# Issuing half of the output stores from ScalarE, half from SyncE, in a vision tower kernel on one core

## What is computed

```python
tokens = layernorm(patches, ln1_g, ln1_b) @ W1 + b1
tokens = layernorm(tokens, ln2_g, ln2_b)
tokens = jnp.concatenate([tokens, tokens, tokens], axis=1)      # (4, 3 * 784, 64)
h = silu(layernorm(tokens @ Wp1 + bp1, lnp_g, lnp_b)) @ Wp2 + bp2
h = h + gated_layer(layernorm(h))
h = h + experts_4(layernorm(h))
# attention, 8 heads of rank 32
scores = einsum('bhtr,bhur->bhtu', q, k) / sqrt(64)
h = h + einsum('bhtd,hde->bte', softmax(scores) @ x, VO)
# experts 1 to 8, the best two weighted
for e in range(8):
    y = gelu(tokens @ w1[e] + b1[e], approximate=False) @ w2[e] + b2[e]
    out = out + combine[:, e:e + 1] * y
return h + out                                                   # (4, 2352, 64)
```

## Time and profile before

| | before |
|---|---|
| median of 3 runs | 721.47 us (716.13 to 722.4) |
| the profiled execution, device time | 709.28 us |
| its span, first to last instruction | 707.5 us |
| outside of the span | 1.8 us |
| TensorE busy | 639.1 us, 90% of the span |
| VectorE, ScalarE, GpSimd busy | 425.3, 353.6, 66.7 us |
| mean granted TensorE clock | 0.972 of full speed |

### The profile page before, as it was taken

How to read it: one execution, slowest core, us unless ns; L and a number is a source line. 1 busy time by engine, 2 the same in 40 slices (tenths; PEclk the granted TensorE clock), 3 DMA queues, 4 the chain that set the end, 5 groups by cost and what they waited for, 6 DMA issues and landing times.

```text
span 707.5 us, 10081 instructions
## 1 busy us (share of the span) xinstructions
PE 639.1 (90%) x3032; PEld 334.3 (47%) x3032; DVE 425.3 (60%) x1028; ACT 353.6 (50%) x538; POOL 66.7 (9%) x76
## 2 busy tenths in 40 slices
PE   0795888997969999999999999999999999978993
PEld 0552444544435555545555555555555554446431
DVE  3845456125857676676677676677676775187451
ACT  0547885648524445445445445455445455568211
POOL 0000000001990010010010010010110100100000
PEclk9998899999979999999999999999999999999997
DMA  7400000001521232231221322322322310000024
GB/s 154 189 0 1 0 0 1 0 1 46 137 63 50 63 75 65 68 84 50 73 77 50 79 71 50 84 65 50 87 62 56 93 50 2 1 1 0 1 51 85
DMA packets 22112, 37.83 MB, mean 53 GB/s; under 512 B 5624, under 2 KB 15288, under 8 KB 21832
## 3 DMA queue, kind: packets, MB, share of 16 engines
q1 hardware_dynamic: 21944, 37.32, 20.8%
q10 hardware_dynamic: 144, 0.20, 0.2%
HBM read 6.27 MB, written 2.61 MB: 13 GB/s over the span
## 4 chain that ended last, share of the span: by engine, by line
PE 86%; DVE 5%; ACT 3%; DMA 3%; SPq 1%; issue 1%; DVEq 0%; ACTq 0%
PE P L662 83%; DMA X<-x 2%; PE P L678 1%; ACT L472 1%; DVE xs L1218 1%; ACT rs L472 0%; PE P L908 0%; PE P L1020 0%; SPq L351 0%; PE P L782 0%; DVE xhat L1158 0%; DVE mx L1328 0%; DVE gate_s L1206 0%; SPq L355 0%; SPq L356 0%
## 5 line engine op out<-in xcount | busy, mean ns | idle before, releaser
L572 ACT ACTIVATE PT<-P 112x784 f32<-112x784 f32 x224 | 184.4, 823 | 215.6 <-PE P L662 215.5
L1328 DVE TENSOR_REDUCE mx<-P 112x1 f32<-112x392 f32 x448 | 243.1, 563 | 80.6 <-PE P L662 80.5
L662 PE MATMUL P<-PT,XVs 112*64 112x392 f32 x896 | 197.4, 519 | 0.2
L662 PE MATMUL P<-Ks,Qs 96*112 96x392 f32 x448 | 171.4, 387 | 1.8 <-DMA Ks<-QKH 1.1
L662 PEld LDWEIGHTS P<-Ks,Qs 96*112 96x112 f32 x448 | 77.4, 175 | 118.3 <-DVE mx L1328 111.6
L662 PE MATMUL P<-Qs,Ks 98*112 98x392 f32 x448 | 118.6, 346 | 6.8 <-DMA Qs<-row_store 6.8
L662 PEld LDWEIGHTS P<-Qs,Ks 98*112 98x112 f32 x448 | 78.4, 178 | 15.3 <-issue 13.1
L662 PEld LDWEIGHTS P<-PT,XVs 112*64 112x64 f32 x896 | 44.4, 135 | 61.7 <-issue 60.9
L662 PEld LDWEIGHTS P<-VBs,CT 128*98 128x98 f32 x320 | 34.8, 165 | 20.2 <-issue 19.0
L1355 DVE RECIPROCAL zi<-P 98x1 f32<-98x1 f32 x32 | 5.4, 168 | 63.5 <-PE P L662 63.5
L662 PE MATMUL P<-VBs,CT 128*98 128x130 f32 (+1 forms) x320 | 39.2, 269 | 0.6 <-ACT CT L579 0.6
(11 more groups left out here) (178 smaller groups left out, 599.9 us busy)
## 6 DMA issues: line engine op xcount, KB each, us to landing
Qs<-QKH SPq DMA_DIRECT2D x64, 98.0 KB, 2.1
Ks<-QKH SPq DMA_DIRECT2D x64, 98.0 KB, 2.2
XVs<-XV SPq DMA_DIRECT2D x32, 196.0 KB, 2.5
Qs<-QKL SPq DMA_DIRECT2D x32, 98.0 KB, 2.1
Ks<-QKL SPq DMA_DIRECT2D x32, 98.0 KB, 2.1
X<-x SPq DMA_DIRECT2D x4, 588.0 KB
out<-OT SPq DMA_DIRECT2D x24, 98.0 KB
wa<-table_a SPq DMA_DIRECT2D x1, 2207.5 KB, 8.2
```

The costliest lines, as they stand in the source:

```text
L572: nc.scalar.activation(PT[:, p, :].rearrange("p (c n) -> p c n", c=2), P[0:T, 2 + 2 * p:4 + 2 * p, 0:HALF], ACT.Exp, scale=float(D) ** -0. ...
L662: return nc.tensor.matmul(dst, lhsT, rhs, start=start, stop=stop, **more)
L1328: nc.vector.tensor_reduce(mx[:, s % 2, c, t:t + 1], bank(c if n is None else n)[0:T, :], AX.X, ALU.max)\
```

## The change

The view of the output is made once, ahead of the engines' blocks, under the name `out_rows`. SyncE keeps the three stores of `j = 0` of each image. The three stores of `j = 1` go to ScalarE's code, right behind the image's two copies, with a wait for ScalarE's own last copy ahead of them. There are 24 stores as before, of the same sizes and to the same places. SyncE still waits for all of them at the end.

```diff
+        out_rows = out.rearrange("b (k i h j cd) d -> b i k h j (cd d)", k=REP, i=NP, h=2, j=OJ)
+
         @block.sync
...
-            rows = out.rearrange("b (k i h j cd) d -> b i k h j (cd d)", k=REP, i=NP, h=2, j=OJ)
             for b in range(B):
                 sync.wait_ge(hid_done, HID["out", b, 1] + 1)
-                for j in range(OJ):
-                    for k in range(REP):
-                        sync.dma_start(rows[b, :, k, :, j, :], OT[j * NP:(j + 1) * NP, b, :, :]).then_inc(stored[b], 16)
+                for k in range(REP):
+                    sync.dma_start(out_rows[b, :, k, :, 0, :], OT[0:NP, b, :, :]).then_inc(stored[b], 16)
...
             for b in range(B):
                 for part in range(2):
                     rows_out_of(b, part)
+                scalar.wait_ge(hid_done, HID["out", b, 1] + 1)
+                for k in range(REP):
+                    scalar.dma_start(out_rows[b, :, k, :, 1, :], OT[NP:2 * NP, b, :, :]).then_inc(stored[b], 16)
```

## The result

| | before | after |
|---|---|---|
| median of 22 runs | 721.67 us (704.48 to 729.11) | 718.84 us (712.57 to 723.57) |
| ratio of medians | | 0.9961 |
| profiled execution | 709.28 us | 718.65 us |
| its span | 707.5 us | 716.8 us |
| mean granted TensorE clock in it | 0.972 | 0.951 |

The comparison of the two kernels gives the ratio 1.0153 (95% interval 1.0102 to 1.0204), so 1.5% slower, while the medians of the same runs say 0.4% faster; it counts only runs within 1.5% of the fastest of their kernel, and these are 2 of the 22 runs of before (704.48 and 709.73 us) against 21 of 22 after.

A forecast was written before the change was run, and what follows sets the result against it. TensorE, busy 639.1 of 707.5 us, bounds the kernel; only the tail can change. Image 3's stores from 698.58, packets 1.6 us later, then 0.9 us: span 704.2, gain 3.3; 721.47 - 3.3 = 718.2 us, range 712.5 to 723.5.

The forecast's parts named there:

- Where the time can change: End of the program: only the 9.4 us behind ScalarE's last copy, 1.3% of the span, can answer to the change.
- the tail: End of the program: from the end of image 2's second copy to the span's end, 12.5 us before the change.
- Images 0 and 1: ScalarE's stores after these images: 2.6 us of issues fit in 7.37 us of idleness, so no gain or loss.
- The delay of image 3's copies: ScalarE after image 2: three issues end at 697.57 us, copies start 0.43 us late, rows ready 0.45 us later.
- The DMA engines decide: Last stores: at a DMA share of 0.9, packets and not issues set the end, 704.2 us, a gain of 3.3.
- Rival A: Last stores: SyncE's and ScalarE's issues exclude each other, image 3's copies wait; span 708.5 us, 1.0 us slower; chance 0.10.
- Rival B: Last stores: packets slow down when two queues feed them, share stays 0.56; span 0.3 us slower, no change; chance 0.10.
- Rival C: Last stores: cheap ScalarE issues, packets overlap fully, issues alone set the end at 702.9 us, gain 4.6 us; chance 0.10.
- The step that failed: From profile to median: the same 3.3 us gain applied 12.2 us higher; scatter alone could pass 1%, slower given 0.03.

## Why the prediction was right and wrong

- **Where the time can change.** Right: the tail only. The changed kernel's profile differs elsewhere, but by the clock, which the kernel before shows alike.
- **Images 0 and 1.** Right: ScalarE's next copy of image 1 still follows 7.37 us of idleness.
- **The delay of image 3's copies.** Forecast 0.43 us, measured 0.56: an interval of 0.89 us on ScalarE, not 0.86. I called it the cost; the kernels that avoid it with stores of this form have longer tails (10.1, 10.4 and 10.2 us).
- **The DMA engines decide.** Right, but the share was 0.79, not the 0.9 taken, so the last packets took 3.4 us and not 3.2. With the later copies this makes the tail 9.6 us where 9.2 was forecast (704.2 less 694.97), a gain of 2.9 us where 3.3 was. By its own terms (698.58 + 1.6 + 3.2 + 0.9) the sum gives 704.3 and not 704.2 us, which changes nothing.
- **Rival A**, the queues exclude each other, is refuted: 0.820 us on SyncE with ScalarE issuing beside it and without, and 0.852 us on ScalarE, with SyncE issuing beside it and, in the kernel with all stores on ScalarE, without. The lock wait that the Trainium skill describes ("Perfetto Trace Analysis", section "DMA Instruction — HWDGE (DVE, Sync)") does not show in these lengths. Rival A's other half, copies queued behind issues, is real, as all stores on ScalarE show.
- **Rival B** is refuted: the DMA share rose from 0.56 to 0.79. The Trainium skill ("DMA: Bandwidth & Descriptors", section "Issuing engines are not separate DMA queues") says that several issuing engines save only issuing time, usually little. The trace agrees that it is issuing time that is saved, but here that is not little: issuing was 0.82 us for a store whose packets need about 0.5 us of the DMA engines, and where issuing was made cheap on one queue, the second queue gained nothing (8.6 against 9.0 us).
- **Rival C**, no bound by the DMA engines, did not come.
- **The time.** 718.2 us was forecast, the median is 718.84 us. Both medians, of the 3 runs known then and of the 22 after, are of the common group of runs, and that they are is luck: the sum did not know of the groups.
- **The step that failed.** The comparison came out at 1.0153, beyond 1% on the slower side, to which I gave 0.03. The step is the last sentence of the sum, "Against the median of the runs, 12.2 us higher, the same gain", with the statement under chances that "no mechanism gives 7.2". I took the 12.2 us between the profiled execution and the median as an offset and the runs as scatter around one value. They are two groups some 12 us apart, set by 10 or 37.5 us of the lower clock near 195 us, and the profiled execution was of the rare one. Each splits by another 5 to 6 us, as 716.13 us among the three runs could have told. The mechanism outside the change that moves a run by 1.7% was in the profile's distance to its own runs, and I did not ask what it was. A comparison that takes the rare group for one kernel and the common one for the other shows that group's distance, less the gain. Why the clock comes back early in some executions stays open.

## What to carry to other kernels

When the last stores are issued without a pause and the DMA engines are not full, the issuing binds; look first at the form of the store, since a store of one row of 1,792 bytes for each partition, with the repeats inside, halved the issue here, and gave more on one queue than a second queue did. A DMA issue on a compute engine stands in its queue: what counts is whether the next work of that engine comes later than the issues end, or whether the packets that it starts earlier are worth the wait. Where a profiled execution lies over 1% from the median of its kernel, find the stretch that differs before any two profiles are compared, and compare runs of the same kind.

## What was not expected of the hardware

- The granted clock stays at the lower level for 10 or for 37.5 us from nearly the same place on, in the same kernel, with TensorE busy for most of the longer one; that is some 12 us of 720.
- The same eight matmuls near 50 us took 5.57 us in one execution and 2.88 us in another, with a granted clock of 1.00 shown in both.
- A store of 28 partitions by 1,792 bytes took 0.39 us to issue, three repeats of it in one 0.40 us, and one with two such rows a partition 0.82 us.
- ScalarE's first store of the program took 1.47 us, later ones 0.85; SyncE's first 1.02, later ones 0.82.
- ScalarE began to issue a store 0.16 us before the copy that stands ahead of it in the program had started (seen once).
